# Two pipelined attentions: a table of places for every step, and an order of its own for each engine

## Reference

```python
x = L0_attn_x                                     # [16, 512, 256], float32
x = x + L0_attn(layernorm(x), Wqkv, Wout)         # 16 heads of 16, rotary, causal window of 128
x = x + L0_ffn(layernorm(x), Wr, br, Wl1, ...)    # 8 experts, top 2 of them for each token
x = x + L1_attn(layernorm(x), Wq, bq, Wk, ...)    # 16 heads of 16, xpos rotary, full causal, biases
x = x + L1_ffn(layernorm(x), weight)              # one ternary matrix, 256 x 256
```

## Time and profile before

| | us |
|---|---|
| median of 3 runs | 2851.01 |
| lowest, highest run | 2846.03, 2851.59 |
| span of the profiled execution | 2865.3 |
| PE busy in it | 2452.9 (86%) |
| DVE busy | 1725.7 (60%) |
| ACT busy | 1349.0 (47%) |
| POOL busy | 894.8 (31%) |

### The profile page before, as it was taken

The page is one execution under the profiler, slowest core; times in us unless marked ns, Lnnn a source line. Parts: engine busy times, 40 slices in busy tenths (PEclk is TensorE's granted clock), DMA queues, the critical chain, the costliest instruction groups (busy, mean ns, idle before and its releaser), DMA issues. The chain is left out here.

```text
span 2865.3 us, 50759 instructions
## 1 busy us (share of the span) xinstructions
PE 2452.9 (86%) x17549; PEld 1683.6 (59%) x17722; DVE 1725.7 (60%) x5775; ACT 1349.0 (47%) x2419; POOL 894.8 (31%) x847
## 2 busy tenths in 40 slices
PE   4688888888889848999999983798999998998996
PEld 3355555555555537989898872455555555555553
DVE  4566676766677635444445435667676677666651
ACT  2355555545455423333333321255655555555654
POOL 1434455444554230000000003344443434444300
PEclk7799999999999978999999995799999999999998
DMA  4466655666555357887877746344455444445320
GB/s 134 142 189 209 191 185 168 207 200 197 186 159 154 92 169 262 282 282 262 286 263 275 248 150 190 115 119 146 124 147 145 134 119 119 124 135 141 119 60 16
DMA packets 259617, 490.21 MB, mean 171 GB/s; under 512 B 25608, under 2 KB 191112, under 8 KB 249416
## 3 DMA queue, kind: packets, MB, share of 16 engines
q1 hardware_dynamic: 241944, 435.23, 48.5%
q0 software_dynamic: 17456, 52.19, 5.4%
HBM read 299.65 MB, written 186.52 MB: 170 GB/s over the span
## 5 line engine op out<-in xcount | busy, mean ns | idle before, releaser
L682 ACT ACTIVATE a_pr<-a_bank 128x512 f32<-128x512 f32 (+1 forms) x1152 | 638.0, 573 | 584.0 <-PE a_bank L1105 282.1
L966 DVE CUSTOM_DVE_ANT_0 a_junk<-a_bank,a_smask 128x256 bf16<-128x256 f32 (+3 forms) x1536 | 652.1, 463 | 383.2 <-PE a_bank L1202 356.8
L1246 PE MATMUL a_bank<-a_pr,a_va 128*32 128x256 f32 (+3 forms) x4096 | 350.8, 419 | 33.7 <-ACT a_pr L682 31.2
L1563 PE MATMUL e_bank<-e_xh,e_under 128*128 128x512 f32 (+1 forms) x1248 | 362.1, 375 | 1.4 <-DVE e_xl L1539 1.4
L1202 PE MATMUL a_bank<-a_kst,a_qst 96*128 96x128 bf16 (+3 forms) x1024 | 265.2, 312 | 47.6 <-DVE a_nmax L961 23.8
L1105 PE MATMUL a_bank<-a_mask,a_identb 128*128 128x128 bf16 (+2 forms) x979 | 283.2, 289 | 0.0
L1228 PE MATMUL a_bank<-a_qst,a_kst 98*128 98x512 bf16 (+3 forms) x1024 | 255.3, 304 | 24.0 <-ACT a_pr L682 23.6
L1563 PEld LDWEIGHTS e_bank<-e_xh,e_under 128*128 128x128 f32 x1248 | 222.6, 189 | 40.5 <-DVE e_xl L1539 1.8
L1563 PE MATMUL e_bank<-e_xl,e_under 128*128 128x512 f32 (+1 forms) x624 | 233.9, 375 | 0.0
L1450 POOL DMA_DIRECT2D results_dram<-e_yt x39 | 29.3, 751 | 612.8 <-DVE e_yt L1518 595.3
L554 POOL DMA_INDIRECT xs<-e_rn,e_row x128 | 126.9, 991 | 292.9 <-ACT a_pr L682 83.0
(11 more groups left out here) (214 smaller groups left out, 5059.2 us busy)
## 6 DMA issues: line engine op xcount, KB each, us to landing
e_under<-ws_dram SPq DMA_DIRECT2D x39, 2048.0 KB, 9.1
a_parts_dram<-a_parts SPq DMA_DIRECT2D x224, 256.0 KB
e_under<-ws_dram SPq DMA_DIRECT2D x39, 1024.0 KB, 6.0
e_under<-a_parts_dram SPq DMA_DIRECT2D x96, 384.0 KB, 6.9
a_kst<-a_parts_dram SPq DMA_DIRECT2D x96, 384.0 KB, 8.8
a_parts_dram<-a_parts SPq DMA_DIRECT2D x32, 768.0 KB
ws_dram<-a_ws SPq DMA_DIRECT2D x24, 1024.0 KB, 7.3
a_qst<-a_parts_dram SPq DMA_DIRECT2D x64, 384.0 KB, 7.8
```

The lines of the kernel that those rows point to most:

```text
L682: nc.scalar.activation(pr[b][:, h:h + per, :], TB_[at % 2][:, 0:per * w].rearrange("p (h w) -> p h w", h=per), ACT.Exp, scale=scale).then_ ...
L966: last = nc.vector.tensor_tensor_reduce(junk[:, at % 2, j * w:(j + 1) * w], SB_[at % 2][:, j * w:(j + 1) * w], smask[:, T - w:T], scale=-1 ...
L1246: last = nc.tensor.matmul(PVB[32 * j:32 * (j + 1), q0:q0 + w], va[i % 2][:, b, (g * HG + j) * VW:(g * HG + j) * VW + 32], pr[b][:, j, :], ...
L1563: last = nc.tensor.matmul(out[:, 0:s.columns], first(s.slot, low)[:, kc, col:col + P], x[s.slot][:, kc, 0:s.columns], start=(p == 0), stop ...
```

## Change

No operation, wait, buffer or transfer is added or removed. What changes is where steps stand:

1. `turn(i)` is replaced by `step_list()`, which reads every position from a table `PLACES`, one for each attention. A name has a first position and a gap between its repetitions.
2. The fills and drains have entries of their own, `EDGES` (turns -3 to 0 and 14 to 17), where a name's place may differ from that of the turns between them.
3. All steps of all turns are sorted in one go, so that a step may have a place below 0 or above 1 and move past the border of a turn. Before, each turn was sorted by itself.
4. T and PV steps of a group lie in a stretch of their own (`main0` to `main3`) with a length of its own, where before they were spread over the turn in proportion to their columns.
5. Each engine sorts the list anew with `LAGS`: on this engine, steps of this kind stand so much later or earlier.

```diff
+PLACES = {
+    "a0": {
+        "main0": (-0.0444, 0.13257), "sums0": (0.1739, 0.0078), "flip0": (0.2083, 0.0002), "scale0": (0.6025, 0.00057),
+        "main1": (0.2281, 0.16639), "sums1": (0.4723, 0.0004), "flip1": (0.5872, 0.02462), "scale1": (0.7232, 0.00025),
+        "main2": (0.5136, 0.255), "sums2": (0.7306, 0.00241), "flip2": (0.8198, 0.00506), "scale2": (0.9111, 0.00019),
+        "main3": (0.7729, 0.02805), "sums3": (0.8839, 0.02005), "flip3": (-0.0224, 0.00967), "scale3": (0.0641, 0.00382),
+        "S0": (0.0207, 0.01296), "S1": (0.2542, 0.01923), "S2": (0.4473, 0.02834), "S3": (0.6872, 0.0314),
...
+        "turn2": (0.4488, 0.00273), "score": (0.6608, 0.00246), "exp2": (0.6953, 0.01414), "place": (0.7844, 0.00273),
...
+        "vcopy": (-0.0301, 0.00853), "minus0": (0.6816, 0.01072), "load": (0.4843, 0.00082), "aggr": (0.8125, 0.00393),
+        "stats": (0.6525, 0.0508), "norm": (0.1535, 0.00171), "turn": (0.2209, 0.00838), "stack": (0.7183, 0.0318),
...
+    },
+    "a1": {
+        "main0": (-0.0096, 0.3088), "sums0": (0.2051, 0.00113), "flip0": (0.3292, 0.01622), "scale0": (0.4066, 0.00171),
...
+        "S0": (0.0488, 0.01816), "S1": (0.2664, 0.01816), "S2": (0.5212, 0.02136), "S3": (0.7574, 0.01882),
...
+        "stats2": (0.1994, 0.00694), "aggr2": (0.2785, 0.00232), "norm2": (0.2747, 0.01033), "y": (0.3071, 0.02303),
...
+        "vcopy": (0.0217, 0.00253), "minus0": (0.684, 0.0136), "load": (0.6906, 0.00166), "aggr": (1.0437, 0.23537),
...
+LAGS = {
+    "a0": {
+        "DVE": {
+            "S": 0.0446, "turn": 0.0698, "minus": -0.0078, "aggr2": 0.0647, "aggr": 0.0579, "rope": -0.0071, "part": 0.1199,
+        },
+        "SP": {
+            "minus": -0.0244,
+        },
...
+    "a1": {
...
+        "SP": {
+            "minus": 0.0534,
+        },
...
-    order = []
-    for i in range(-2, B + 2):
-        order += merged([turn(i)])
+    places, edges, lags = PLACES[name], EDGES[name], LAGS[name]
+    timed_steps = step_list()
+    order = merged([timed_steps])
+
+    def order_of(engine):
+
+        late = lags.get(engine, {})
+        return merged([[(pos + late.get(st[0], 0.0), st) for pos, st in timed_steps]])
+
...
-            for st in order:
+            for st in order_of("SP"):
```

More of the change, by code:

```diff
@@ new lines @@
+LAGS = {
+    "a0": {
+        "DVE": {
+            "S": 0.0446, "turn": 0.0698, "minus": -0.0078, "aggr2": 0.0647, "aggr": 0.0579, "rope": -0.0071, "part": 0.1199,
+        },
+        "SP": {
+            "minus": -0.0244,
+        },
+        "ACT": {
+            "back": -0.0049, "turn2": 0.0138, "turn": -0.0452, "part": 0.0419, "T": -0.0055, "minus": -0.0061,
+        },
+        "POOL": {
+            "aggr": 0.0025, "rope": -0.0031, "aggr2": -0.1282, "part": 0.066,
+        },
+    },
+    "a1": {
+        "DVE": {
+            "rope": -0.0001, "minus": -0.0627, "bias": -0.2088, "quantise": -0.1579, "part": -0.0681, "S": 0.0088,
+            "aggr2": -0.0442, "aggr": 0.0343, "turn": 0.0224,
+        },
+        "POOL": {
+            "aggr2": 0.0061, "aggr": 0.0645, "part": 0.0964, "rope": 0.1237,
+        },
+        "ACT": {
+            "turn": 0.01, "part": -0.0174, "back": -0.0097, "turn2": 0.0004, "minus": 0.0211, "T": 0.0013,
+        },
+        "SP": {
+            "minus": 0.0534,
+        },
+    },
+}
@@ L153, in main_steps @@
     def main_steps(i):
-        units = [(g, b) for g in range(NG) for b in range(NT)]
         t_of = {b: [k for k, st in enumerate(t_steps) if st[0] == b] for b in range(NT)}
[L158 to L168, removed]
-        return out
-    def turn(i):
-        s, m, o = i + 1, i + 2, i - 1
+        def scores(g, b):
+            return [(t_steps[k][2] * t_steps[k][4] + 256, ("T", i, g, k)) for k in t_of[b]]
+        out = []
+        for g in range(NG):
+            timed = scores(g, 0) if g == 0 else []
+            for b in range(NT):
+                nxt = scores(g, b + 1) if b + 1 < NT else scores(g + 1, 0) if g + 1 < NG else []
+                timed += nxt[:1] + [(4 * p_width[b], ("PV", i, g, b))] + nxt[1:]
+            total, at = sum(c for c, _ in timed), 0
+            out.append([])
+            for c, st in timed:
+                out[-1].append(((at + c / 2) / total, st))
+                at += c
@@ L173, in turn, with step_list @@
+        return out
+    def step_list():
         out = []
[L174 to L187, removed]
-            if routed:
[L189 to L213, removed]
-            if mixed:
[L215 to L242, removed]
@@ new lines, in step_list @@
+        for n in range(B):
+            i = n - 3
+            put(i, "load", ("load", n))
+            put(i, "aggr", ("aggr", n))
+            row(i, "stats", [("stats", n, t) for t in range(NT)])
+            if mixed:
+                for k in range(2):
+                    row(i, "gather" + str(k), [("gather", n, k, t) for t in range(NT)])
+                    row(i, "mix" + str(k), [("mix", n, k, t) for t in range(NT)])
+        return out
+    places, edges, lags = PLACES[name], EDGES[name], LAGS[name]
@@ L518, in _ @@
                 constants()
-            for st in order:
+            for st in order_of("POOL"):
                 if st[0] == "rest":
@@ L604, in _ @@
             nc.scalar.copy(wh[:, :, :], w_raw).then_inc(wh_done, 1)
-            for st in order:
+            for st in order_of("ACT"):
                 if st[0] == "high":
@@ L722, in _ @@
             dve.wait_ge(wl_done, 1)
-            for st in order:
+            for st in order_of("DVE"):
                 if st[0] == "bias":
@@ L1107, in _ @@
             pe.wait_ge(ident_loaded, 16)
-            for st in order:
+            for st in order_of("PE"):
                 if st[0] == "bias":
```

132 lines of the change are left out of this document (added), and 80 rows, old and new, of tables (EDGES, PLACES).

## The result

The changed kernel takes 2712.16 us (median of 4 runs, 2709.81 to 2714.14), the kernel before beside it 2851.3 (4 runs): a ratio of 0.9505, interval 0.9485 to 0.9525. That is 139 us less, where 101 were forecast; the time lies inside the range, near its low end.

What follows compares the result with a forecast made beforehand. PE's work was taken to bound the turns, leaving its idle time, a0's half clock and part of the fills and drains to win. a0 -69, a1 -22, fills and drains -10 made -101: 2851 to 2750 us, range 2699 to 2815.

Steps and rivals of the forecast that it cites:

- Maxima's DMA, -2.1 a turn: In a0, PE's wait for the DMA of the maxima goes, 2.1 us less a turn.
- Drains -0.7, flips -1.2, projection -1.0: In a0, PE's waits for S drains, flips and projection fall by 0.7, 1.2 and 1.0 us a turn.
- Exps +0.5: In a0, denser groups of T steps make PE wait longer for exps, 0.5 us more a turn.
- Clock, -1.6: In a0, PE's half-clock time falls along with its waits, 1.6 us less a turn.
- my rival: In a0, bunched S and T steps keep PE's clock where it is, losing 18 us: 2768; chance 0.08.
- The quarter kept back: Only three quarters of a0's sum of -6.1 us a turn counted, -4.6, as not all terms add.
- What is late next: In a0, DVE is late next: its longest hold between two drains grows from 2.5 us to 3.5.
- Fills and drains, -10: The four stretches outside the steady turns get 10 us shorter, with +15 and -40 as ends.
- a1, -1.5 a turn: Second attention: exps +0.6 and -0.9, S steps -0.7, scattered rest -0.5, together 1.5 us less a turn.
- queue and flips only: Rival: a0 gets 2.7 us a turn, all else goes back to the next engine: 2811; chance 0.15.
- Slower by exps: Rival: exp waits at the two T banks grow in a0 and a1, making it slower: 2880; chance 0.13.
- the special form under "nothing": In a1, the maxima's DMA behind the second `store` costs 2.1 us a turn: 2781; "nothing" had chance 0.04.

Runs made afterwards that it cites:

- The repaired kernel: The changed kernel with a1's first `mix` steps moved to 0.715 and second gathers to 0.83 of the turn; 2712.23 us (0.9434), later 2698.19 us (0.9424).

## Why the prediction was right

It came out as forecast in sign and place, and 38 us too small. Against the profiled execution, -101 was forecast and -153 came: the turns of a0 gave 97.8 us for 69, the fills and drains of a0 29.6 for 10 in all, a1 26 for 22. Some 15 of the 153 us belong to the traced execution of before: against the old a0 in the kernel with only a1 changed, the turns gave 83.8 and the fills and drains of a0 28.1.

- **Maxima's DMA, -2.1 a turn.** As forecast: no entry left in the waits. But adding this alone gave 12 us where -2.1 x 15 is 31, and removing it alone cost 53.
- **Drains -0.7, flips -1.2, projection -1.0.** By the waits of nine turns: drains 1.9 to 1.1, flips and transposes of the maxima 1.7 to 0.6, projection 1.3 to 0. Close, each.
- **Exps +0.5.** Wrong in sign: 0.8 to 0.7. The sum over pairs of steps rose by 1 us a turn and told nothing about these waits.
- **`turn2`, +1.3.** Missed. It stands in the rows of after as the longest entry.
- **Clock, -1.6.** PE's busy time fell by 2.9 a turn on the traced pair, near the far end that I gave (-3.0), but by 1.5 against the other trace of the old a0 (clock 0.96 there, 0.95 and 0.99 in the pair). So the term was right by the one trace and little more than half of what came by the other. The Trainium skill (TensorE: Matmul & The Clock Gate, "A second HAM failure mode: psum-queue depth-cycling") tells of a clock that swings between its levels when PE idles briefly and often between groups of matmuls that cycle through PSUM banks. In a0 the traces fit it: the bunched groups ran at 0.99 with 4.2 us of idle time a turn, and with T's groups in the old order, 14.8 us a turn, at 0.87. In a1 they don't: 5.8 us a turn in short waits at 1.00 before, 4.2 with one wait of 2.9 at 0.97 after. That bunching by itself keeps the clock down, as my rival had it, is excluded by the 0.99.
- **The quarter kept back.** This is a mis-sized term. The sum of the waits without it was -4.5 a turn; idle time fell by 4.4, or 4.5 against the other trace. It isn't a plain sum: over the nine turns of each, all listed waits of PE but the one before `turn2` fell from 72.4 to 21.4 us, 5.7 a turn, more than forecast, and the new one gave 1.3 back. In all, a0's turns gave 97.8 us, or 83.8, where 6.1 x 15 = 92 was the sum without the quarter and 69 with it. I kept the quarter because a removed wait lets PE run into the next one. The runs show that this happens, and far more than by a quarter, to an edit done alone (12 us for 31). My working compared two whole orders, so the moves of the next producers were in it already; that this is why little was given back here is argued, no run shows it alone.
- **What is late next.** I named DVE's longest hold. In the kernel with the DMA moved alone it was POOL: the scatters ahead of `aggr2`'s scalars, then `norm2` and the exps on ACT. I had noted that the scatters find the last stack earlier and gave that no price.
- **Fills and drains, -10.** From the start to the first score it was 29.0 us less, from the last score to the experts 0.6. The far end given was -40 for all four fills and drains. This is the other mis-sized term: the fill of a0 has places of its own in `EDGES`, which I had not worked out, and no run changed them alone.
- **a1, -1.5 a turn.** Measured -1.3, from other parts: exps 2.4 to 0.4 us a turn (forecast -0.3), drains 1.2 to 0.4, and the new wait in `mix`, +2.9, of which the prediction says nothing. The forecast hit by two errors that cancel. That is luck. The repaired kernel shows what was hidden: -5.6 a turn.

Of the rivals, "queue and flips only" (2811) describes what those edits do alone, 2823, and not the change. "Slower by exps" is excluded by 0.7 and 0.4 us of exp waits a turn, and the special form under "nothing" by the list of a1's waits, which has none for the maxima's DMA.

## What to carry to other kernels

Price a reordering as one piece, by the waits that the new order leaves, and don't expect its parts to add: here the same move was worth 12 or 53 us by what stood around it, and the placing of T cost 119 us when it was put into the old order and up to 103 when it was taken out of the new one. When one wait goes, follow the queues of every engine that its release feeds, POOL's small scalars behind a row of scatters included, to the next one. And after a reordering read the list of waits for entries that are new: the one in a1 was 2.9 us a turn, and moving two kinds of steps gave 49 us.

## What the runs showed of the hardware

The same a0 took different times from execution to execution. The experts started at 957.06 in the changed kernel and at 957.76 in the one with only a0 changed, but at 1007.5, 997.99 and 995.82 in three later ones with the same a0, in sets where the kernel before was only 16 and 11 us slower than in the first. Timeline of DVE at the end of `aggr` and the first drain behind it, in the changed kernel's first execution and in its second:

```profile
415.61 0.37 DVE L1019 BATCH_NORM_AGGREGATE a_mv<-a_stats 128x2 f32<-128x6 f32 x4
415.90 0.27 DVE L1184 CUSTOM_DVE_ANT_0 a_junk<-a_bank,a_smask 128x128 bf16<-128x128 f32 x1
```

```profile
421.75 0.37 DVE L1019 BATCH_NORM_AGGREGATE a_mv<-a_stats 128x2 f32<-128x6 f32 x4
425.43 0.29 DVE L1184 CUSTOM_DVE_ANT_0 a_junk<-a_bank,a_smask 128x128 bf16<-128x128 f32 x1 [3.31 <-remote]
```

At this one place DVE stands still for 2 to 3 us, in 12 of the turns by its list of waits:

```profile
DVE a_junk L1184 <- remote: 29.7, 12, 3.3
```

What DVE waits for there the trace doesn't name: PE had begun the S step at 421.58, and such a step takes it 0.4 us. Over the nine turns PE's wait for drains grows from 9.6 to 29.3 us, but its wait before `turn2`, 11.6, is gone, so only 6.0 of the 16.3 us that nine turns are longer (497.70 for 481.40) are idle time of PE; the other 10.3 are busy time, at clock 0.98 for 0.99. Most of the rest of the 41 us lies in a0's last turns, where the clock was 0.85 for 0.89.

It isn't a matter of the new order or of the later sets alone. The repaired kernel has it in both its traces (32.9 and 26.6 us) and the kernel with the DMA behind the stacks too (26.4). So has the traced execution of before, whose list of DVE's waits from 200 to 1000 says:

```profile
DVE a_junk L966 <- remote: 16.9, 9, 2.5
```

The two kernels of the first set with one attention changed have none of it, one with the old a0 and one with the new. Why it appears in some executions and not in others is open, and with it how much of the ratio's difference, 0.9505 and 0.9598 for one kernel, it explains.
